# A routed layer whose units run in two phases of token tiles

## The reference, cut to what matters

```python
logits = jnp.clip(xt @ gate_w.T, -50.0, 50.0)     # xt: layer norm of x, [2048, 512]
top_w, top_idx = jax.lax.top_k(logits, 2)
rw = jax.nn.softmax(top_w, axis=-1)
vals = jnp.einsum('tk,tks->ts', rw, weighted[top_idx])   # 4096 masked weights per expert
contrib = segment_sum((xt[:, cols] * vals).T, rows, num_segments=512)
x = x + tanh(g_ffn[1]) * (xt @ W.T + contrib.T)
```

## Time and profile before

| | |
|---|---|
| median of three runs | 2045.58 us |
| the profiled execution | 2045.0 us, span 2043.3 us |
| granted TensorE clock, mean | 0.947 |
| stage `routed_maps` | from 1822.7 us to the end |
| first matmul of unit 0 | 1876.4 us |
| last `scaled` begins | 2003.8 us |
| last add begins | 2036.7 us |

### The profile page before, as it was taken

How to read it: one execution, slowest core, us unless ns; L and a number is a source line. 1 busy time by engine, 2 the same in 40 slices (tenths; PEclk the granted TensorE clock), 3 DMA queues, 4 the chain that set the end, 5 groups by cost and what they waited for, 6 DMA issues and landing times. The chain is left out here.

```text
span 2043.3 us, 38716 instructions
## 1 busy us (share of the span) xinstructions
PE 1836.0 (90%) x11488; PEld 1411.4 (69%) x11488; DVE 1181.0 (58%) x2665; ACT 925.6 (45%) x2631; POOL 961.7 (47%) x1018
## 2 busy tenths in 40 slices
PE   5889999999978999999999999994789999886992
PEld 3555666566547999999999999982455566555881
DVE  6866777677654875333333353325777778764445
ACT  5466767676642332233333333321466666640110
POOL 2557877788641364043333443322455555212660
PEclk9789999999998999999999999997899999996996
DMA  9677787778757246589999986533444545539657
GB/s 301 236 230 231 243 279 239 220 240 282 236 170 279 80 132 212 161 233 273 324 328 268 275 261 192 119 59 107 92 109 104 118 100 119 127 104 365 235 163 277
DMA packets 234941, 414.82 MB, mean 203 GB/s; under 512 B 44361, under 2 KB 121457, under 8 KB 228986
## 3 DMA queue, kind: packets, MB, share of 16 engines
q1 hardware_dynamic: 168250, 323.86, 49.7%
q0 software_dynamic: 30592, 62.54, 13.2%
q10 hardware_dynamic: 35904, 25.96, 4.2%
HBM read 211.97 MB, written 157.82 MB: 181 GB/s over the span
## 5 line engine op out<-in xcount | busy, mean ns | idle before, releaser
L963 ACT ACTIVATE a_P<-a_SC,a_nm 128x256 f32<-128x256 f32 x512 | 235.9, 473 | 151.5 <-DVE a_nm L845 150.9
L1543 POOL DMA_INDIRECT b_y_rows<-b_ysb,b_entry x79 | 125.0, 1582 | 334.8 <-ACT b_ysb L1691 185.0
L845 DVE TENSOR_REDUCE a_nm<-a_SC 128x2 f32<-128x512 f32 x256 | 164.7, 685 | 127.8 <-PE a_SC L1147 127.7
L673 POOL TENSOR_TENSOR a_praw<-a_praw,a_phigh 128x704 f32<-128x704 f32 (+2 forms) x126 | 193.8, 1538 | 10.3
L1795 DVE TENSOR_TENSOR b_xl<-b_XT,b_xh 128x512 fp32r<-128x512 f32 x97 | 67.0, 691 | 216.1 <-ACT b_xh L1697 215.7
L1158 PEld LDWEIGHTS a_T<-ident,a_P 128*128 128x128 f32 x1024 | 121.4, 146 | 86.5 <-issue 46.4
L1158 PE MATMUL a_T<-ident,a_P 128*128 128x128 f32 x1024 | 149.5, 285 | 26.8 <-DVE a_PT L857 24.1
L671 POOL CAST a_phigh<-a_praw 128x704 fp32r<-128x704 f32 (+2 forms) x126 | 106.5, 845 | 107.1 <-DMA a_praw<-in_L_ffn_wd 33.4
L1801 DVE TENSOR_TENSOR b_al<-b_AT,b_ah 128x384 fp32r<-128x384 f32 x111 | 61.8, 557 | 152.6 <-ACT b_ah L1702 152.6
L2529 ACT ACTIVATE c_P<-c_SC,c_nm 128x240 f32<-128x240 f32 x256 | 115.7, 457 | 75.6 <-DVE c_P L2400 75.6
L1691 ACT ACTIVATE b_ysb<-b_Y 128x512 f32<-128x512 f32 x79 | 47.3, 599 | 223.1 <-PE b_Y L1638 211.6
(11 more groups left out here) (496 smaller groups left out, 4916.4 us busy)
## 6 DMA issues: line engine op xcount, KB each, us to landing
w_parts<-a_phigh SPq DMA_DIRECT2D x72, 352.0 KB, 3.6
w_parts<-a_praw SPq DMA_DIRECT2D x72, 352.0 KB, 4.1
b_wh<-w_parts SPq DMA_DIRECT2D x18, 1216.0 KB, 10.9
b_wl<-w_parts SPq DMA_DIRECT2D x18, 1216.0 KB, 14.4
c_q<-c_qT SPq DMA_DIRECT2D x64, 256.0 KB
c_k<-c_kT SPq DMA_DIRECT2D x124, 128.0 KB
b_wh<-w_parts SPq DMA_DIRECT2D x18, 704.0 KB, 5.2
b_wl<-w_parts SPq DMA_DIRECT2D x18, 704.0 KB, 7.8
```

The costliest lines, as they stand in the source:

```text
L673: eng.tensor_tensor(raw[:, 0:k * m], raw[:, 0:k * m], r32(high[:, 0:k * m]), ALU.subtract).then_inc(plow_done, 1)
L845: eng.tensor_reduce(nm[:, g % 4, j, :], SC[j][:, :].rearrange("p (t k) -> p t k", t=BT), AX.X, ALU.max, negate=True).then_inc(topped, 1)
L963: e = eng.activation(Pr[:, i, t, :], SC[j][:, t * S:(t + 1) * S], ACT.Exp, bias=nm[:, g % 4, j, t:t + 1], accum_out=den[:, h, t:t + 1])
L1543: eng.indirect_dma_start(out=y_rows, out_offset=bass.IndirectOffsetOnAxis(ap=entry[:, r, 1:2].bitcast(U32), axis=0), in_=ysb[:, v % RING, ...
```

## The change

The picks of token tiles 0 to 7 (EARLY = 8) are placed first, expert by expert, each expert's part rounded up to whole units. The picks of tiles 8 to 15 fill what is left of their expert's early units and then take further units, again expert by expert. NR stays 39 and every unit's work is the same. The early picks need at most 23 units, so after the scatter of unit 22 all rows of tiles 0 to 7 are in `y_rows`. The loads, adds and stores of these eight tiles are issued during units 23 to 36, one tile at a time in two sets of four buffers; `added` at the end runs for tiles 8 to 15 alone. The kept sums are loaded once for tiles 8 to 13 (1.5 MB), and tile by tile for 0 to 7.

```diff
+    EARLY = NT // 2
+    EARLY_UNITS = (EARLY * P * K + E * (BLOCK - 1)) // BLOCK
+    EARLY_AT = {EARLY_UNITS + 3 + 3 * i // 2: i for i in range(EARLY)}
+    STAGES = 2
@@ sync, after the wait for SUMS_AFTER units
-            for first, n, a in SUMS:
-                eng.dma_start(a, core.x_rows[first * P:(first + n) * P, :].rearrange("(t p) d -> p t d", p=P)
-                              ).then_inc(sums_in, 16)
+            eng.dma_start(core.Xa[:, RING:RING + kept, :],
+                          core.x_rows[EARLY * P:HOME * P, :].rearrange("(t p) d -> p t d", p=P)).then_inc(sums_in, 16)
+            def early_loads(i):
+                for a, rows in zip(staged(i), (core.x_rows[rows_of(i), :], y_rows[rows_of(i), :], y_rows[rows_of(NT + i), :])):
+                    eng.dma_start(a, rows).then_inc(early_in[i % STAGES], 16)
+
+            for i in range(RING):
+                eng.wait_ge(y_sent[i], 16 * ((EARLY_UNITS - 1 - i) // RING + 1))
+            for i in range(STAGES):
+                early_loads(i)
+            for i in range(EARLY):
+                eng.wait_ge(early_added, i + 1)
+                eng.dma_start(of[rows_of(i), :], staged(i)[3]).then_inc(early_kept[i % STAGES], 16)
+                if i + STAGES < EARLY:
+                    early_loads(i + STAGES)
             for i in range(RING):
                 eng.wait_ge(y_sent[i], 16 * ((NR - 1 - i) // RING + 1))
-            for q in range(NG):
+            for q in range(EARLY // GT, NG):
@@ tensor, count_chosen
+                    if t < EARLY:
+                        eng.matmul(R[:, (NT + 1) * E:], ones[:, :], mask[:, t, :], start=False, stop=False)
@@ vector, places
-                eng.tensor_tensor(nb_p[:, :, :], tri[:, :, :], nb_i[:, :].unsqueeze(1).to_broadcast([P, E, E]),
+                eng.tensor_tensor(nb_p, co[:, :, :], nb_i[:, :].unsqueeze(1).to_broadcast([P, 2 * E, 2 * E]),
                                   ALU.mult).then_inc(vseq, c.inc())
+                eng.tensor_tensor(over_cap, R[:, EARLY * E:NT * E].rearrange("p (t e) -> p t e", e=E),
+                                  nb_i[:, E:2 * E].unsqueeze(1).to_broadcast([P, NT - EARLY, E]),
+                                  ALU.is_ge).then_inc(vseq, c.inc())
...
+                eng.tensor_tensor(over_cap, over_cap, base[:, E:2 * E].unsqueeze(1).to_broadcast([P, NT - EARLY, E]),
+                                  ALU.mult).then_inc(vseq, c.inc())
...
+                eng.tensor_tensor(at[:, EARLY:NT, :], at[:, EARLY:NT, :], over_cap, ALU.add).then_inc(vseq, c.inc())
@@ vector
+            def added_early(i):
+                summand, first_rows, second_rows, total = staged(i)
+                eng.wait_ge(early_in[i % STAGES], 16 * 3 * (i // STAGES + 1))
+                ge(eng, early_kept[i % STAGES], 16 * (i // STAGES))
+                eng.tensor_tensor(total, first_rows, second_rows, ALU.add).then_inc(vseq, c.inc())
+                eng.wait_ge(vseq, c.now)
+                eng.tensor_tensor(total, total, summand, ALU.add).then_inc(early_added, 1)
@@ vector, in the loop over units
                 scaled(r)
-            eng.wait_ge(sums_in, 16 * len(SUMS))
-            for t in range(NT):
+                if r in EARLY_AT:
+                    added_early(EARLY_AT[r])
+            eng.wait_ge(sums_in, 16)
+            for t in range(EARLY, NT):
                 added(t)
```

More of the change, by code:

```diff
@@ L2774, in routed_maps @@
     SUMS_AFTER = 12
-    CONSTS = 12
+    EARLY = NT // 2
+    EARLY_UNITS = (EARLY * P * K + E * (BLOCK - 1)) // BLOCK
+    EARLY_AT = {EARLY_UNITS + 3 + 3 * i // 2: i for i in range(EARLY)}
+    STAGES = 2
+    CONSTS = 17
+    assert EARLY <= NT - GT and max(EARLY_AT) < NR
     assert NR <= 64 and BLOCK == P
@@ L2806, in routed_maps @@
         ex, s1 = sb("ex", [P, NT]), sb("s1", [P, NT])
-        tri = sb("tri", [P, E, E])
+        co = sb("co", [P, 2 * E, 2 * E])
         mask = sb("mask", [P, NT, E], BF16)
         earlier, ones = sb("earlier", [P, P], BF16), sb("ones", [P, P], BF16)
-        none = sb("none", [P, (NT + 1) * E], BF16)
+        none = sb("none", [P, (NT + 2) * E], BF16)
         first_i, first = sb("first_i", [P, E], I32), sb("first", [P, E])
@@ L2815, in routed_maps @@
         code_w = sb("code_w", [P, PICKS, 2])
-        nb_i, base, end = sb("nb_i", [P, E], I32), sb("base", [P, E]), sb("end", [P, E])
-        nb_p = sb("nb_p", [P, E, E])
+        nb_i, base = sb("nb_i", [P, 2 * E], I32), sb("base", [P, 2 * E])
+        end = m2
         at, at_k, at_i = sb("at", [P, NT, E]), sb("at_k", [P, PICKS]), sb("at_i", [P, PICKS], I32)
@@ L2850, in routed_maps @@
             sem(n) for n in ("rows_turned", "rows_high", "rows_low", "y_done", "y_scaled")]
-        sums_in = sem("sums_in")
+        sums_in, early_in = sem("sums_in"), [sem(f"early_in{i}") for i in range(STAGES)]
+        early_added, early_kept = sem("early_added"), [sem(f"early_kept{i}") for i in range(STAGES)]
         y_sent = [sem(f"y_sent{i}") for i in range(RING)]
@@ L2870, in low, with staged @@
             return unit_parts[:, r % 2, 1]
-        SUMS = ((0, GT, back[:, :, :]), (GT, BT, xs[:, :, :]), (RING, HOME - RING, core.Xa[:, RING:HOME, :]))
+        kept = HOME - EARLY
+        spare = [a[:, i, :] for a, i in [(back, i) for i in range(GT)] + [(xs, i) for i in range(BT)]
+                 + [(core.Xa, i) for i in range(RING + kept, HOME)]]
+        assert len(spare) >= 4 * STAGES
+        def staged(i):
+            return spare[4 * (i % STAGES):4 * (i % STAGES) + 4]
         def sums_of(t):
-            for first, n, a in SUMS:
-                if first <= t < first + n:
-                    return a[:, t - first, :]
-            return core.Xa[:, t, :]
+            return core.Xa[:, RING + t - EARLY if t < HOME else t, :]
         @block.sync
@@ L2904, in _, with rows_of @@
             eng.wait_ge(y_done, SUMS_AFTER)
-            for first, n, a in SUMS:
-                eng.dma_start(a, core.x_rows[first * P:(first + n) * P, :].rearrange("(t p) d -> p t d", p=P)
-                              ).then_inc(sums_in, 16)
+            eng.dma_start(core.Xa[:, RING:RING + kept, :],
+                          core.x_rows[EARLY * P:HOME * P, :].rearrange("(t p) d -> p t d", p=P)).then_inc(sums_in, 16)
+            of = out.rearrange("b s d -> (b s) d")
+            def rows_of(t):
+                return slice(t * P, (t + 1) * P)
+            def early_loads(i):
[10 more added lines that the diff above has]
+                    early_loads(i + STAGES)
             for i in range(RING):
                 eng.wait_ge(y_sent[i], 16 * ((NR - 1 - i) // RING + 1))
-            for q in range(NG):
+            for q in range(EARLY // GT, NG):
                 for k in range(K):
@@ L2913, in _ @@
                     eng.dma_start(choice(k, q), rows.rearrange("(t p) d -> p t d", p=P)).then_inc(parts_in[q], 16)
-            of = out.rearrange("b s d -> (b s) d")
-            for t in range(0, NT, 2):
-                eng.wait_ge(out_ready, t + 2)
+            for t in range(EARLY, NT, 2):
+                eng.wait_ge(out_ready, t + 2 - EARLY)
                 eng.dma_start(of[t * P:(t + 2) * P, :].rearrange("(t p) d -> p t d", p=P),
                               choice(0, t // GT)[:, t % GT:t % GT + 2, :]).then_inc(stored, 16)
-            eng.wait_ge(stored, 16 * NT // 2)
+            for i in range(STAGES):
+                eng.wait_ge(early_kept[i], 16 * (EARLY // STAGES))
+            eng.wait_ge(stored, 16 * (NT - EARLY) // 2)
         @block.gpsimd
@@ L2934, in _ @@
             eng.iota(pad_i[:, :], pattern=[[BLOCK, NR]], base=K * T + 1, channel_multiplier=1).then_inc(consts, 1)
-            eng.wait_ge(consts, CONSTS - 2)
-            eng.affine_select(out=tri[:, :, :], in_=tri[:, :, :], compare_op=ALU.is_gt, fill=0.0, base=0,
-                              pattern=[[1, E], [-1, E]], channel_multiplier=0).then_inc(consts, 1)
+            eng.wait_ge(consts, CONSTS - 4)
             eng.affine_select(out=earlier[:, :], in_=earlier[:, :], compare_op=ALU.is_gt, fill=0.0, base=0,
                               pattern=[[1, P]], channel_multiplier=-1).then_inc(consts, 1)
+            before = [[1, E], [-1, E]]
+            for block_, fill in ((co[:, 0:E, E:2 * E], 0.0), (co[:, E:2 * E, 0:E], 0.0), (co[:, E:2 * E, E:2 * E], 1.0)):
+                eng.affine_select(out=block_, in_=block_, compare_op=ALU.is_gt, fill=fill, base=0, pattern=before,
+                                  channel_multiplier=0).then_inc(consts, 1)
+            eng.wait_ge(consts, CONSTS)
+            eng.affine_select(out=co[:, E:2 * E, E:2 * E], in_=co[:, E:2 * E, E:2 * E], compare_op=ALU.not_equal,
+                              fill=0.0, base=0, pattern=before, channel_multiplier=0).then_inc(coefs, 1)
             def gather(r):
@@ L2997, in count_chosen @@
                 for t in range(a, b):
-                    eng.matmul(R[:, (t + 1) * E:].rearrange("p (t e) -> p t e", e=E), ones[:, :],
```

(25 more changed lines are left out.)

19 lines of the change are left out of this document (13 added, 6 removed).

## The result

The changed kernel has a median of 2033.18 us in four runs (2032.22 to 2037.14), the kernel before 2045.96 us in its four (2042.79 to 2046.41): ratio 0.9942, interval 0.9921 to 0.9963. The forecast was 2034.3, and faster. The traced execution took 2033.88 us, span 2032.2 us.

The account below looks back on a forecast made before the run. PE bounds the units, VectorE and DMA together the end. 2045.0 - 10.8 (adds) - 1.5 (last store) + 0.2 (second pair) + 0.8 (early transfers) = 2033.7 against the profiled execution, 2034.3 us against the median; range 2031.5 to 2039.5.

Parts of the forecast that it names:

- The end: After the last unit: eight tile adds go (10.8 us), second pair costs 0.2, last store lands 1.5 sooner (bounds 0 and 1.9).
- the second pair's wait: At the end, 2.1 MB of loads come 5.4 us after the first pair, when VectorE has done four tiles; 0.2 us allowed.
- Placement and units' order: Before unit 0 and in the first units: longer `places` (1.1 us) and maps wanted sooner, taken to cost 0.
- the 0.4 us to spare: Before unit 0: its first matmul waited 1.46 us for SP, so 1.1 us more on the gathers' path stays hidden.
- Early adds on VectorE: In the later units: two operations, 1.35 us, behind `scaled`, making 2.8 of 3.2 us per unit; hidden.
- the slack of 2.4 us: In the units: an early add waiting up to 2.4 us for data costs nothing through VectorE's low part.
- Early transfers: Beside units 23 to 36: 217 GB/s asked of the bulk queue's 234, 93% full; cost 0.8 us, bounds 0 and 6.
- The gathers: In the units: a gather landing in 6.7 us beats its transposes by 0.6 us; stalls begin when an add waits 0.9 us.
- GpSimd's hold: Rival 1, in the units: early adds delay GpSimd's scatter and next gather by 1.1 us; +3 us, 2037; chance 0.15.
- Late tiles, the second rival: In the units: bulk rate falls below 217 GB/s with stores, tiles come late; 3 to 6 us, 2037 to 2040; chance 0.11.
- slow landing: Rival 3, early loads: landing time sets a buffer set's turn; at 13 us landing the time is 2050; chance 0.03.
- slower end: Rival 4, at the end: tile 7's late store or add, or a later first pair, holds it; about 2045; chance 0.03.

Follow-up runs that it names:

- order-only kernel: Changed kernel with the two-phase placement kept but loads, adds and stores of all sixteen tiles back at the end: 2044.28 us beside 2043.72 of the kernel before.
- adds-only kernel: Changed kernel with early adds kept, one load of eight buffers behind unit 12 replacing the 24 loads and 8 stores; tiles 0 to 7 not written: 2032.22 us.
- transfers-only kernel: Changed kernel with its early loads, stores and VectorE's waits but without the sixteen adds; tiles 0 to 7 get the kept sums' rows: 2034.48 us.

## Why the prediction was right, step by step

- **The end.** Forecast: -10.8 for the adds, +0.2 for the second pair's wait, -1.5 for the last store. Measured: -10.3 for the first two together, with a wait of 0.43 us, and -1.8. The first add came 0.2 us later, for which the forecast had 0. That both resources had to be halved together shows in the second pair's wait: VectorE and the transfers still end within half a microsecond of each other.
- **Placement and units' order.** Forecast 0; the order-only kernel gives 0.85 us before unit 0 and no wait for maps. The mis-sized step is the 0.4 us to spare: it takes TensorE to be ready as soon as unit 1's transposes have ended. In the changed kernel its wait for SP is down from 1.46 us to 0.40, and the first matmul begins 1.5 us after unit 1's transposes do, where unit 1's rows had just come. So the 1.1 us on VectorE's path reached unit 0 in part: 0.7 us, more than the 0.5 that the prediction had named as the sign of this part being wrong. All kernels with the new order have 0.4 to 1.0 us. Two rows of its timeline:

```profile
1872.80 0.72 PEld L3057 LDWEIGHTS d_XT<-ident,Xa 128*128 128x128 f32 x4 [0.42 <-DMA Xa<-b_xn_rows,d_token_i]
1874.32 0.79 PE L3073 MATMUL d_Y<-d_Mh,d_unit_parts 128*128 x1 [0.40 <-SPq L2912]
```

- **Early adds on VectorE.** Hidden, as forecast, and the slack of 2.4 us was right: waits of up to 2.3 us cost nothing, waits of 2.9 and 3.0 cost 0.5 and 0.6.
- **Early transfers.** The queue model was near: 24 loads landed in 3.1 to 8.4 us, and only two adds waited, 0.9 us each at most. From 1958 to 1998 the bulk queue moved 7.29 MB, 182 GB/s, less than the 217 that the prediction wanted of it. Of the two other traces of these units, one has adds waiting 3.9 us in all (up to 1.5), the other 2.5 (up to 1.2).
- **The gathers.** This is the step that was mis-sized: 0.8 us taken, bounds 0 and 6, for the losses behind the early work; measured 3.2, 2.0 and 1.1 in three traces (3.5, 2.3 and 1.7 with what the step into unit 15 lost more than before). I put the margin at 0.6 us, from the landing of 6.7 us to the transposes, and let stalls begin with an add that waits. Both halves were off. Landings went to 7.6 us in traffic that lasted 40 us in place of 16. And what has to be in time is not the transpose but the queue's next entry, the register load behind it; what should have warned is that the kernel before already lost 0.13 us in the step into unit 15, beside its load of the kept sums.
- **Rivals.** GpSimd's hold is there with 0.19 us, not 1.1. Late tiles, the second rival, are there by their sign, adds that wait for early loads, but without the 3 to 6 us of cost: in the changed kernel the waits stayed within the slack. The slow landing and the slower end didn't come.
- **A part that no step had.** 2.8 us of the traced difference lie before the stage, inside the spread between executions. Inside the stage the change is worth 8 to 9 us (220.3 to 212.0 and 210.9); the medians differ by 11.6 and 12.8. Whether all of the rest is that spread is open: the kernel before has one trace only. That the traced execution met its forecast to 0.2 us (2033.9 against 2033.7) is luck: the units cost 2.7 us more than was taken, and 2.8 us came from before the stage. Without these last 2.8 it would have been 2036.7 us, still faster and inside the range. The mechanism of the gain, the moved adds and transfers at the end, was right; two of the prediction's own signs, units every 3.216 us throughout and no wait for a gather, failed.

## What to carry to other kernels

Work moved under a busy engine is paid for in the prefetches that share its resource: before filling the DMA engines beside a pipeline, count the lead of every prefetch with the landing under load, and give it one more buffer's lead if one is free (here the units took 122.2 to 123.0 us in three traces with it and 124.0 to 125.8 in three without). On an engine's queue, whatever stands behind a wait is late with it; put register loads that don't need the awaited data ahead of the wait. When the last stage of a kernel waits for a first transfer, its size sets the start, down to the point at which later pieces no longer arrive in time.

## What the runs showed that was not expected

- A wait for rows that ended 0.3 us before its transposes were due still cost 1.0 us, through the register load behind it; with the load ahead of the wait the units lost 1.0 us, against 1.7 to 3.5 (one trace against three).
- An indirect scatter issued while VectorE adds two SBUF operands takes 1.18 us on GpSimd, else 0.97 to 1.02, in 8 of 8 such units of the adds-only kernel and in none of the transfers-only kernel.
- A pair of 1 MB loads was in 8.3 us after the first issue, a pair of 0.5 MB after 5.3.
